# Two layers of attention and feed-forward: the experts' up projections in three single-pass products of high and low parts

## The reference

```
probs = softmax(xt @ Wg); eidx = argmax(probs); gate = probs at eidx
pos = place of the row among the rows of its expert; keep = pos < C
xd = rows scattered to (expert, place), zeros elsewhere          # E x C x 256
h = silu(xd @ W1) * (xd @ W3);  oe = h @ W2                      # per expert
out = oe at the row's place * gate * keep
shared = silu(xt @ sw1) * (xt @ sw3) @ sw2
result = x + out + shared
```

## Time and profile before

| | us |
|---|---|
| median of 3 runs | 1689.48 |
| lowest, highest | 1689.08, 1689.71 |
| span of the profiled execution | 1686.7 |

### The profile page before, as it was taken

One profiled execution on the slowest core, in us unless ns is written; L12 is line 12 of the kernel. 1 busy time (PEld: TensorE's weight loads), 2 busy tenths in 40 slices (PEclk: granted clock), 3 DMA queues, 4 the chain that ended last, 5 costly groups with the idle time before them and its releaser, 6 DMA issues. The chain is left out here.

```text
span 1686.7 us, 48689 instructions
## 1 busy us (share of the span) xinstructions
PE 1618.2 (96%) x16127; PEld 1295.4 (77%) x16127; DVE 1318.1 (78%) x3043; ACT 1013.4 (60%) x2024; POOL 1015.6 (60%) x970
## 2 busy tenths in 40 slices
PE   5889999999999999999999999999899889999998
PEld 4668888888888888888888888888787545555787
DVE  6988888888888888888888888888794668885223
ACT  5776666666666666666666666666332356664121
POOL 5348787878787878787878877787300124431321
PEclk8599999999999999999999999999999999999999
DMA  9721121121121122112112112512850011101244
GB/s 254 251 72 43 50 77 44 42 84 42 44 70 56 42 59 67 44 48 78 42 50 76 44 42 83 119 44 66 200 120 1 7 41 64 64 8 52 98 144 158
DMA packets 184808, 125.97 MB, mean 75 GB/s; under 512 B 107562, under 2 KB 171992, under 8 KB 184368
## 3 DMA queue, kind: packets, MB, share of 16 engines
q1 hardware_dynamic: 183216, 121.27, 26.2%
q0 software_dynamic: 1536, 3.99, 0.6%
HBM read 81.98 MB, written 24.48 MB: 63 GB/s over the span
## 5 line engine op out<-in xcount | busy, mean ns | idle before, releaser
L1175 POOL TENSOR_TENSOR c_rest<-c_prob 128x1024 f16<-128x1024 f32 (+1 forms) x513 | 796.1, 1572 | 242.8 <-ACT c_prob L964 232.6
L964 ACT ACTIVATE c_prob<-c_psS,ln,c_exp_scale 128x1024 f32<-128x1024 f32 (+1 forms) x514 | 536.4, 1044 | 241.2 <-PE c_psS L800 236.2
L1069 DVE TENSOR_REDUCE c_mxp<-c_psM 128x1 f32<-128x400 f32 (+1 forms) x1040 | 588.8, 573 | 113.7 <-PE c_psM L784 96.8
L800 PE MATMUL c_psS<-c_q,c_kk 128*128 128x256 f16 (+1 forms) x3350 | 512.6, 272 | 0.2 <-issue 0.2
L818 PE MATMUL c_psV<-c_vb,c_prob 128*128 128x129 f16 (+1 forms) x3328 | 396.5, 222 | 0.8 <-ACT c_acc L1018 0.8
L800 PEld LDWEIGHTS c_psS<-c_q,c_kk 128*128 128x128 f16 (+1 forms) x3350 | 321.8, 99 | 85.7 <-issue 0.4
L821 PE MATMUL c_psV<-c_vb,c_rest 128*128 128x65 f16 (+1 forms) x3328 | 374.2, 193 | 0.0
L784 PE MATMUL c_psM<-c_kkm,c_q 128*128 128x400 f16 (+1 forms) x1040 | 346.1, 333 | 4.8 <-DVE c_mxp L1069 3.0
L821 PEld LDWEIGHTS c_psV<-c_vb,c_rest 128*128 128x128 f16 (+1 forms) x3328 | 301.4, 99 | 22.1
L818 PEld LDWEIGHTS c_psV<-c_vb,c_prob 128*128 128x128 bf16 (+1 forms) x3328 | 305.3, 97 | 15.4 <-ACT c_acc L1018 1.1
L746 PE MATMUL c_psQ<-c_xb,c_w2s 128*128 128x256 f16 x1188 | 164.1, 275 | 6.0 <-PEq L163 4.2
(11 more groups left out here) (322 smaller groups left out, 2192.2 us busy)
## 6 DMA issues: line engine op xcount, KB each, us to landing
c_w2s<-w_scr SPq DMA_DIRECT2D x66, 256.0 KB, 2.6
c_ms<-m_scr SPq DMA_DIRECT2D x67, 192.0 KB, 2.3
c_w2s<-w_scr SPq DMA_DIRECT2D x66, 128.0 KB, 2.0
acc_scr<-c_acc SPq DMA_DIRECT2D x129, 64.0 KB
kv<-acc_scr SPq DMA_DIRECT2D x16, 512.0 KB, 6.6
m_w<-in_L_ffn_W SPq DMA_DIRECT2D x16, 352.0 KB, 3.5
c_vb<-V SPq DMA_DIRECT2D x27, 129.0 KB, 2.0
c_kk<-KK SPq DMA_DIRECT2D x27, 128.0 KB, 2.0
```

The source lines that it names most:

```text
L800: mm = pe.matmul(psS[g % 2][0:r, i * S:(i + 1) * S], src[:, (lo + i) * P:(lo + i) * P + r], mov[slot][:, :], start=(one == 0 and i % 2 == ...
L964: nc.scalar.activation(prob[g][0:r, 0:w], psS[g % 2][0:r, 0:w], ACT.Exp, bias=keep["ln1024"][0:r, :], scale=exp_scale[slot][0:r, :]).then_ ...
L1069: nc.vector.tensor_reduce(mxp[:, st, c:c + 1], psM[:, st, 0:CHUNKS[c][1]], AX.X, ALU.max).then_inc(mx_done, 1)
L1175: nc.gpsimd.tensor_tensor(rest[g][0:r, 0:w], prob[g][0:r, 0:w], high[0:r, 0:w], ALU.subtract).then_inc(rest_done, 1)
```

## The change

The up projections of all 16 tiles are computed from operands of type float32r (fp32 rounded for the matrix unit), each fp32 operand split in a high part (the rounded value) and a low part (what is left). `hidden` gives three matmuls for each fp32 matmul of before: high weights by high columns, high weights by low columns, low weights by high columns. The product of the two low parts is left out.

The parts are made by the other engines. ScalarE copies to the high part: the shared weights at the start (`swh`), each expert's weights (`high_weights`), each shared tile's columns (`high_tile`) and the turned expert's rows (`high_columns`, in place of `columns`). GpSimd subtracts the high part from the fp32 value for the weights (`low_weights`) and the shared tiles (`low_tile`), at the start, between the scatters of the rows, and ahead of the scatters of the results. VectorE does so for the experts' rows (`low_columns`). TensorE waits for the low parts. SyncE loads the weights of expert e as soon as the low weights of e - 2 are made.

```diff
@@ -2292,7 +2293,11 @@
     w1 = [sb(f"w1_{i}", [P, DK, HID]) for i in range(2)]
     w3 = [sb(f"w3_{i}", [P, DK, HID]) for i in range(2)]
     w2 = [sb(f"w2_{i}", [P, FTN, D]) for i in range(2)]
-    xt = [sb(f"xt{i}", [P, DK, CAP1]) for i in range(2)]
+    swh, swl = sb("swh", [P, 2, DK, HID], F32R), sb("swl", [P, 2, DK, HID], F32R)
+    wh = [sb(f"wh{i}", [P, 2, DK, HID], F32R) for i in range(2)]
+    wl = [sb(f"wl{i}", [P, 2, DK, HID], F32R) for i in range(2)]
+    mh = [sb(f"mh{i}", [P, DK, CAP1], F32R) for i in range(2)]
+    ml = [sb(f"ml{i}", [P, DK, CAP1], F32R) for i in range(2)]
...
     scattered = sem("scattered")
-    xt_full, xt_done = sem("xt_full"), sem("xt_done")
+    xt_full = sem("xt_full")
+    swh_done, swl_done = sem("swh_done"), sem("swl_done")
+    wh_done, wl_done = sem("wh_done"), sem("wl_done")
+    mh_done, ml_shared, ml_own = sem("mh_done"), sem("ml_shared"), sem("ml_own")
     h_full, silu_done, g_done = sem("h_full"), sem("silu_done"), sem("g_done")
...
             for e in range(2, E1):
-                sp.wait_ge(h_full, FTN * (HEAD + e - 2) + FTN)
+                sp.wait_ge(wl_done, 2 * e - 2)
...
         @block.gpsimd
         def _(pool):
+            def low_tile(n, k):
+                pool.wait_ge(mh_done, n + 1)
+                i = n if n < HEAD else HEAD + k
+                nc.gpsimd.tensor_tensor(ml[n % 2][:], xT[:, :, i * CAP1:(i + 1) * CAP1], mh[n % 2][:].bitcast(F32),
+                                        ALU.subtract).then_inc(ml_shared, 1)
+
+            def low_weights(e):
+                for k, w in enumerate((w1, w3)):
+                    pool.wait_ge(wh_done, 2 * e + k + 1)
+                    nc.gpsimd.tensor_tensor(wl[e % 2][:, k], w[e % 2][:], wh[e % 2][:, k].bitcast(F32),
+                                            ALU.subtract).then_inc(wl_done, 1)
+
+            for k, w in enumerate((sw1, sw3)):
+                pool.wait_ge(swh_done, k + 1)
+                nc.gpsimd.tensor_tensor(swl[:, k], w[:], swh[:, k].bitcast(F32), ALU.subtract).then_inc(swl_done, 1)
+            low_tile(0, 0)
+            low_tile(1, 0)
+            low_weights(0)
+            low_tile(2, 0)
             pool.wait_ge(in_z, 256)
             pool.wait_ge(named, 1)
             pool.wait_ge(gates_ready, 1)
@@ -2395,7 +2422,17 @@
                     out=t["xd_scr"], out_offset=bass.IndirectOffsetOnAxis(ap=s_idx[:, j:j + 1], axis=0),
                     in_=rows[:, j, :], in_offset=None, bounds_check=E1 * CAP1 - 1, oob_is_err=False
                 ).then_inc(scattered, 16)
+                if j == NT // 4:
+                    low_tile(3, 0)
+                if j == 3 * NT // 4:
+                    low_tile(4, 0)
+            low_tile(5, 0)
+            low_weights(1)
             for e in range(E1):
+                if e + 2 < E1:
+                    low_weights(e + 2)
+                else:
+                    low_tile(HEAD + e + 2, e + 2 - E1)
...
         @block.tensor
         def _(pe):
-            def hidden(n, a1, a3, moving, part):
+            def hidden(n, high, low, part):
 
                 for f in part:
                     f0, fw = FT1[f]
                     slot = psH[f]
                     pe.wait_ge(g_done, FTN * n + f + 1)
-                    for k, a in enumerate((a1, a3)):
+                    for k in range(2):
+                        out = slot[0:fw, k * CAP1:(k + 1) * CAP1]
                         for c in range(DK):
-                            mm = pe.matmul(slot[0:fw, k * CAP1:(k + 1) * CAP1], a[:, c, f0:f0 + fw],
-                                           moving(c), start=(c == 0), stop=(c == DK - 1))
+                            a, b = high[:, k, c, f0:f0 + fw], low[:, k, c, f0:f0 + fw]
+                            pe.matmul(out, a, mh[n % 2][:, c, :], start=(c == 0), stop=False)
+                            pe.matmul(out, a, ml[n % 2][:, c, :], start=False, stop=False)
+                            mm = pe.matmul(out, b, mh[n % 2][:, c, :], start=False, stop=(c == DK - 1))
                     mm.then_inc(h_full, 1)
...
-                moving = (lambda c: xT[:, c, i * CAP1:(i + 1) * CAP1] if isinstance(i, int) else
-                          xT[:, c, bass.ds(i * CAP1, CAP1)])
-                hidden(n, sw1, sw3, moving, (0,))
+                pe.wait_ge(ml_shared, i + 1)
+                hidden(n, swh, swl, (0,))
                 if last is not None:
...
-                hidden(n, sw1, sw3, moving, (1,))
+                hidden(n, swh, swl, (1,))
                 if n == HEAD - 1:
                     transposes(0)
-                hidden(n, sw1, sw3, moving, (2,))
+                hidden(n, swh, swl, (2,))
             def transposes(e):
                 pe.wait_ge(in_xd[e], 16)
-                pe.wait_ge(xt_done, e + 1)
+                if e > 0:
+                    pe.wait_ge(ml_own, e)
...
             def own(e, last):
                 u = e % 2
-                pe.wait_ge(in_w[u], 32 * (e // 2) + 32)
-                pe.wait_ge(xt_done, e + 2)
-                hidden(HEAD + e, w1[u], w3[u], lambda c: xt[u][:, c, :], (0,))
+                pe.wait_ge(wl_done, 2 * e + 2)
+                pe.wait_ge(ml_own, e + 1)
+                hidden(HEAD + e, wh[u], wl[u], (0,))
...
-                hidden(HEAD + e, w1[u], w3[u], lambda c: xt[u][:, c, :], (1, 2))
+                hidden(HEAD + e, wh[u], wl[u], (1, 2))
...
             pe.wait_ge(turned_out, 5)
-            hidden(0, sw1, sw3, lambda c: xT[:, c, 0:CAP1], (0,))
+            pe.wait_ge(swl_done, 2)
+            pe.wait_ge(ml_shared, 1)
+            hidden(0, swh, swl, (0,))
...
-            hidden(0, sw1, sw3, lambda c: xT[:, c, 0:CAP1], (1, 2))
+            hidden(0, swh, swl, (1, 2))
...
-            def columns(e):
+            def high_tile(n, k=0):
+                i = n if n < HEAD else HEAD + k
+                act.wait_ge(turned_out, i + 1)
+                if n >= 2:
+                    act.wait_ge(h_full, FTN * (n - 2) + FTN)
+                nc.scalar.activation(mh[n % 2][:], xT[:, :, i * CAP1:(i + 1) * CAP1], ACT.Copy).then_inc(mh_done, 1)
+
+            def high_columns(e):
                 act.wait_ge(xt_full, e + 1)
+                act.wait_ge(h_full, FTN * (HEAD + e - 2) + FTN)
+                nc.scalar.activation(mh[e % 2][:].rearrange("p c s -> p (c s)"), psH[3][:],
+                                     ACT.Copy).then_inc(mh_done, 1)
+
+            def high_weights(e):
+                act.wait_ge(in_w[e % 2], 32 * (e // 2) + 32)
                 if e >= 2:
                     act.wait_ge(h_full, FTN * (HEAD + e - 2) + FTN)
-                nc.scalar.activation(xt[e % 2][:].rearrange("p c s -> p (c s)"), psH[3][:],
-                                     ACT.Copy).then_inc(xt_done, 1)
+                for k, w in enumerate((w1, w3)):
+                    nc.scalar.activation(wh[e % 2][:, k], w[e % 2][:], ACT.Copy).then_inc(wh_done, 1)
...
-            for k in range(TURNED, NT // 2 - 1):
+            act.wait_ge(in_s, 64)
+            nc.scalar.activation(swh[:, 0], sw1[:], ACT.Copy).then_inc(swh_done, 1)
+            drain_rows(TURNED)
+            nc.scalar.activation(swh[:, 1], sw3[:], ACT.Copy).then_inc(swh_done, 1)
+            for k in range(TURNED + 1, NT // 2 - 1):
                 drain_rows(k)
+            high_tile(0)
             for q in range(len(score_slots) - 1):
                 drain_scores(q)
             drain_rows(NT // 2 - 1)
             drain_scores(len(score_slots) - 1)
+            high_tile(1)
             silu(0, 0)
             act.wait_ge(l_done, 2)
             nc.scalar.activation(ex[:], ex[:], ACT.Exp).then_inc(ex_ready, 1)
-            act.sem_inc(xt_done, 1)
+            high_weights(0)
             for n in range(1, HEAD + E1):
+                if HEAD <= n < HEAD + E1 - 1:
+                    if n > HEAD:
+                        high_weights(n - HEAD + 1)
                 silu(n, n % 2, (0,))
                 if HEAD - 1 <= n < HEAD + E1 - 1:
-                    columns(n - HEAD + 1)
+                    high_columns(n - HEAD + 1)
+                else:
+                    high_tile(n + 1, n + 1 - HEAD - E1)
                 silu(n, n % 2, (1, 2))
-            for n, _ in TAILS:
-                silu(n, n % 2)
+                if n == HEAD - 2:
+                    high_weights(1)
+            for k, (n, _) in enumerate(TAILS):
+                silu(n, n % 2, (0,))
+                if k + 1 < len(TAILS):
+                    high_tile(n + 1, k + 1)
+                silu(n, n % 2, (1, 2))
...
+
+            def low_columns(e):
+                dve.wait_ge(mh_done, HEAD + e + 1)
+                nc.vector.tensor_tensor(ml[e % 2][:].rearrange("p c s -> p (c s)"), psH[3][:],
+                                        mh[e % 2][:].bitcast(F32).rearrange("p c s -> p (c s)"),
+                                        ALU.subtract).then_inc(ml_own, 1)
...
             for n in range(2, HEAD):
                 gated(n, n % 2, (0,))
```

(8 more changed lines are left out.)

## The result

The changed kernel took 1685.99 us, median of 8 runs (1682.52 to 1686.54), against 1689.58 us for the kernel before beside it. The ratio is 0.9972, 95% interval 0.9962 to 0.9982: a gain of 3.6 us, where 9.5 were forecast, and just inside the forecast's range (1673.5 to 1686.0). The profiled execution took 1683.52 us, its span 1681.7.

What follows compares the result with a forecast made beforehand. TensorE, busy 96% of the span, was taken as the bound. +1.0 before expert 0, -9.5 experts, -1.0 tail gave -9.5 from the profiled 1686.7 us: 1677.2, plus 2.8 to the median, 1680.0 us; range 1673.5 to 1686.0.

Steps and rivals of the forecast that it cites:

- I take 111 ns: TensorE's new up-projection passes: assumed spacing per pass, ends 107 and 216 ns; a tile 3.99 us, 1.19 us saved per tile.
- the experts' term: Eight experts' tiles, each 1.19 us shorter if the weights are ready: 9.5 us saved, an expert taking 7.03 us.
- Rival B: Expert stage: GpSimd becomes the bound, 7.55 us an expert, 3.6 us less saved, 1683.6 us; chance 0.20.
- The start: Up to the scatter: GpSimd's subtractions delay VectorE's small operations; last turn 0.9 us late, first scatter 0.65 us later.
- the 13 operations walked through: VectorE's last tiles' normalisation beside three GpSimd operations: two slip through, the third waits; end 1544.2, not 1541.8.
- Between the scatters: Low parts of tiles 3 and 4 queue behind GpSimd's scatters: TensorE stalls 5.3 and 5.2 us; expert 0 starts 1.0 us later.
- The tail: After the last expert: TensorE's 2.4 us saved ends in the wait for the rows read back; 1.0 us credited.
- 3.93 us gap: TensorE's pause at 1578.20 in the kernel before, followed by a down projection of 4.54 us and not 2.60.
- rival A: VectorE and GpSimd operations don't hold each other up: scatter starts at 1561.0, sum -13 us, 1676.5 us; chance 0.24.
- rival C: TensorE's new passes stream like fp32 records, 216 ns each: +36 us, 1725 us; chance 0.08.

## Why the prediction was wrong in size

The sum was +1.0 (up to expert 0), -9.5 (experts), -1.0 (tail). In the recorded traces expert 0 starts at 65.58 and not 62.54, +3.0. From there to `down` of expert 7 it is 60.2 us and not 67.0, -6.9. The rest is 18.23 and not 18.74, -0.5. Together -4.3, 5.2 short of the forecast. The other 0.8 us to the median of 1686.0 lie outside the stage.

- **"I take 111 ns"** is the first step that failed, the largest term mis-sized. 119.0 ns make a tile 4.28 us, not 3.99; an expert's period is 7.30, not 7.03. Eight times 0.27 us are 2.2 of the 2.65 us missing in the experts' term. The row chosen (16 gathers at 112 ns) has 128 columns moving of another type; its load (192 ns) and its record (275 ns) are as long as here (189 and 282), and the spacing is not the same. A spacing for an operand type that no row has deserved a case of its own between 107 and 216 ns, not a point value.
- **Rival B** took part: weights late. In the changed kernel's trace periods of 7.58, 7.45 and 7.54 us stand among the 7.30 (0.7 us in sum), on chip 3 8.02, 7.97 and 7.95 (2.0 us). On chip 3 ScalarE waited 3.02 us for the load of the weights, GpSimd starts the pair of subtractions at 1622.70, and TensorE waits for the second:

```profile
1622.70 3.36 POOL L2406 TENSOR_TENSOR m_wl<-m_w,m_wh 128x704 fp32r<-128x704 f32 x2 [4.70 <-ACT m_wh L2603]
...
1626.12 0.39 PE L2456 MATMUL m_psH<-m_mh,m_wh 128*128 128x256 f32 x1 [0.44 <-POOL m_wl L2406]
```

- **The start.** The mechanism was right and the working of it short: the last turn was forecast 0.9 us late and is 2.0. Three VectorE operations wait for GpSimd, not one; they lose 3.6 us together. (The step of the inverse root also has three rounds, not the two of the 13 operations walked through, but it has them in both kernels.)
- **Between the scatters.** The stall at tile 3 came as told (5.3 forecast, 4.66). The second is 1.67 and not 5.2 us, in the main because TensorE came to it late: it ran at a granted clock of 0.50 behind the first and took 2.93 us for 12 passes in place of 1.43, and 3.99 us for `down` in place of 2.60. For that 0.9 us stood in the sum, at the second gap; it was 2.9, at the first. A late silu (1585.91) added the pause of 0.87 us.
- **The tail.** 0.5 of the 1.0 us came. Without the read back the tail is 0.7 to 1.2 us shorter; even so the chain ends in VectorE's operations of 1.2 us on the rows, which the working of the tail left out.
- **What no step had: the 3.93 us gap was taken as the kernel's own.** With its slow `down` it is 5.9 us of the recorded 148.30 (142.44 without). In the changed kernel GpSimd's stalls stand in its place, so there they replace a loss that was there before, and the change gained. Where the kernel before has no gap, the same stalls are new: against 142.44 the changed kernel's 143.47 to 145.55 are slower. Forecast and result both compare with a pause that other chips do not have. That the sign was right, and the median just inside the range, was luck: on chip 3 there was no gain to see, and on chip 5 the forecast would have been wrong in sign.
- **Right:** the prices of all operand parts, 576 passes, VectorE's small operations held up by GpSimd's (so rival A fell), and no sign of rival C.

## What to carry to other kernels

A pause in a trace is first to be looked for in a second trace on another chip: a change that hides behind it gains nothing once it is gone. Work for an idle engine is not free when it holds up the engine on the path. Here three edits together (the subtractions for the shared weights and six tiles moved from the idle GpSimd to the busier VectorE, expert 0's put behind the scatters, the parts in fp16) turned a loss of 2.0 us into a gain of 10.9 on one chip. A type whose spacing no row shows gets a range, and its two-byte neighbour is to be tried.

## What the runs showed of the hardware

- A VectorE operation of two columns takes 0.16 us alone and 1.2 to 1.6 us beside a GpSimd subtraction, and ends with it; subtractions whose result nobody reads do it as well (1.52 and 1.12 us).
- The same products in three passes cost 119.0 ns each with round fp32 parts and 109.4 ns with fp16 parts, the weight loads 189 and 98 ns.
- While the second eight of 16 indirect scatters are issued, and up to 2.5 us behind them, ScalarE's operations come up to 8.7 us late (1586.92 for a product of 1578.20) in some executions and on time in others, of one and the same kernel. In one trace VectorE's are late there too (idle for 2.0 us with its product ready). The cause is open.
- The granted clock of the program's first 100 us differs between executions (0.80 or 0.64 from 50 to 100 us); with it the stage's start moves by up to 2.8 us.
